# Attention steps with the transposes of a pair's probabilities ahead of the next pair's scores

## The reference

```python
q = (x @ wq).reshape(b, n, H, DH).transpose(0, 2, 1, 3)      # H = 16 heads of DH = 64
sim = jnp.einsum('bhid,bhjd->bhij', q, k) * SCALE
sim = jnp.where(mask[:, None, None, :], neg, sim)
attn = jax.nn.softmax(sim, axis=-1)
out = jnp.einsum('bhij,bhjd->bhid', attn, v)
return out.transpose(0, 2, 1, 3).reshape(b, n, INNER) @ wo + bo
```

## Time and profile before

| what | value |
|---|---|
| time, median of 3 runs | 1245.56 us (1244.93 to 1246.37) |
| the profiled execution's own time | 1244.36 us |
| its span, first to last instruction | 1242.6 us |
| TensorE busy | 1218.9 us (98%) |
| VectorE busy | 995.5 us (80%) |
| ScalarE busy | 875.4 us (70%) |
| GpSimd busy | 705.0 us (57%) |
| chain that ended last | TensorE 78%, VectorE 7%, ScalarE 5%, GpSimd 4% |

### The profile page before, as it was taken

The page is one execution under the profiler, slowest core; times in us unless marked ns, Lnnn a source line. Parts: engine busy times, 40 slices in busy tenths (PEclk is TensorE's granted clock), DMA queues, the critical chain, the costliest instruction groups (busy, mean ns, idle before and its releaser), DMA issues.

```text
span 1242.6 us, 31390 instructions
## 1 busy us (share of the span) xinstructions
PE 1218.9 (98%) x10415; PEld 1165.9 (94%) x10415; DVE 995.5 (80%) x2685; ACT 875.4 (70%) x2261; POOL 705.0 (57%) x1100
## 2 busy tenths in 40 slices
PE   8899999999999999999999999899999999999998
PEld 6899999999999999999999999899999999999898
DVE  6898988988989988888888888754454888888964
ACT  5788887888888888878878877544333776777642
POOL 4676656656678856555555578876515222334451
PEclk9999999999999999999999999999999999999999
DMA  6060000000000003200000010010004677877722
GB/s 195 2 244 22 2 18 19 2 18 19 2 27 27 2 27 121 77 27 27 2 27 27 2 36 27 27 49 30 1 20 152 224 267 270 267 247 249 264 82 92
DMA packets 74383, 100.60 MB, mean 81 GB/s; under 512 B 5616, under 2 KB 53616, under 8 KB 74224
## 3 DMA queue, kind: packets, MB, share of 16 engines
q1 hardware_dynamic: 72688, 94.40, 23.1%
q0 software_dynamic: 1536, 4.20, 1.1%
HBM read 84.16 MB, written 14.42 MB: 79 GB/s over the span
## 4 chain that ended last, share of the span: by engine, by line
PE 78%; DVE 7%; ACT 5%; issue 4%; POOL 4%; DMA 1%; POOLq 0%; DVEq 0%; ACTq 0%
PE ps_pj L52 9%; PE ps_pj L54 9%; PE ps_pj L53 9%; PE ps_t L949 8%; PE ps_s L939 8%; PE ps_pv L962 8%; PE ps_aux L52 3%; PE ps_aux L54 3%; PE ps_aux L53 3%; ACT probs L1268 3%; PE ps_s L52 3%; PE ps_s L54 3%; PE ps_s L53 3%; PE ps_pv L54 2%; PE ps_pv L53 2%
## 5 line engine op out<-in xcount | busy, mean ns | idle before, releaser
L666 POOL TENSOR_SCALAR probs<-probs,inv 128x256 f32<-128x256 f32 x512 | 237.2, 483 | 224.1 <-DVE inv L1512 223.4
L1268 ACT ACTIVATE probs<-scores,nb 128x256 f32<-128x256 f32 x512 | 253.6, 497 | 18.4 <-DVE nb L1502 17.9
L1502 DVE CUSTOM_DVE_ANT_0 scores<-ps_s,maskf 128x256 f32<-128x256 f32 x512 | 186.8, 421 | 51.3 <-PE ps_s L939 49.2
L1275 ACT ACTIVATE probs_t_hi<-ps_t 128x512 fp32r<-128x512 f32 x256 | 150.8, 590 | 103.4 <-PE ps_t L949 103.4
L1516 DVE TENSOR_TENSOR probs_t_lo<-ps_t,probs_t_hi 128x512 fp32r<-128x512 f32 x256 | 173.1, 676 | 0.2
L949 PE MATMUL ps_t<-ident,probs 128*128 128x128 f32 x1024 | 139.9, 279 | 0.6 <-POOL probs L666 0.6
L962 PE MATMUL ps_pv<-probs_t_lo,v_stack 128*128 128x256 f32 x512 | 130.6, 287 | 0.8 <-issue 0.7
L962 PE MATMUL ps_pv<-probs_t_hi,v_stack 128*128 128x256 f32 x512 | 127.8, 282 | 0.0
L949 PEld LDWEIGHTS ps_t<-ident,probs 128*128 128x128 f32 x1024 | 109.7, 141 | 17.8 <-POOL probs L666 0.9
L52 PE MATMUL ps_pj<-xq_hi,wq_lo 128*128 128x256 f32 x368 | 115.3, 313 | 3.3 <-POOL wk_lo L713 3.2
L685 POOL TENSOR_TENSOR heads_t_lo<-joined,heads_t_hi 128x256 fp32r<-128x256 f32 x128 | 95.1, 743 | 33.4 <-ACT heads_t_hi L1284 33.0
(11 more groups left out here) (285 smaller groups left out, 4480.6 us busy)
## 6 DMA issues: line engine op xcount, KB each, us to landing
raw<-in_L_ffn_W SPq DMA_DIRECT2D x96, 512.0 KB, 4.7
slot_rows<-hin SPq DMA_DIRECT2D x3, 768.0 KB, 5.9
rows<-in_x SPq DMA_DIRECT2D x8, 256.0 KB, 2.7
after_self<-rows SPq DMA_DIRECT2D x8, 256.0 KB, 2.1
rows<-after_self SPq DMA_DIRECT2D x8, 256.0 KB, 2.8
cin<-in_ctx SPq DMA_DIRECT2D x8, 256.0 KB, 3.0
after_cross<-rows SPq DMA_DIRECT2D x8, 256.0 KB, 2.2
stage<-in_L_xattn_fc_w SPq DMA_DIRECT2D x2, 1024.0 KB, 9.3
```

The source lines that it names most:

```text
L666: last = pool.tensor_scalar(PR[:, h, t, :], PR[:, h, t, :], inv[:, h, t:t + 1], 1.0, ALU.mult, ALU.mult)
L1268: last = act.activation(PR[:, h, t, :], SM[:, h, t, :], ACT.Exp, bias=nb[:, h, t:t + 1], scale=-1.0, accum_out=sums[:, h, t:t + 1])
L1275: act.activation(flat(PT[0][:, i % 2, h, :, :]), ps_t[h][:, :], ACT.Copy).then_inc(t_hi, 1)
L1502: last = dve.tensor_tensor_reduce(SM[:, h, t, :], ps_s[h][:, t * S:(t + 1) * S], maskf[:, i // PAIRS % 2, :], -SCALE, -LOWEST, ALU.add, AL ...
```

## The change

In steps 2 to 126 of TensorE's loop, the scores of the next pair are issued behind the two transposes of this pair's probabilities, not ahead of them. Steps 0, 1 and 127 keep the order. The other engines' queues are the same.

```diff
@@ -1165,7 +1165,8 @@
             for i in range(NPAIR + 3):
                 if i == 1:
                     project_qk(i + 2)
-                if i + 1 < NPAIR:
+                turned_first = 2 <= i < NPAIR - 1
+                if i + 1 < NPAIR and not turned_first:
                     scores(i + 1)
                 if i == 0:
                     project_qk(i + 2)
@@ -1177,6 +1178,8 @@
                 if i < NPAIR:
                     transpose_probs(i, 0)
                     transpose_probs(i, 1)
+                if turned_first:
+                    scores(i + 1)
                 if i >= 2 and i + 2 < NPAIR:
                     project_qk(i + 2)
                 if i >= 4 and i % 2 == 0:
```

## The result

The changed kernel takes 1345.88 us (median of 4 runs, 1344.22 to 1346.06) against 1245.82: a ratio of 1.080, 95% interval 1.078 to 1.082. Slower by 100 us, where 82 were forecast. The profiled execution took 1345.81 us, with a span of 1344.1.

The account below looks back on a forecast made before the run. TensorE's order bounds the kernel; after the change, a loop of 1.28+0.81+3.87+0.06+0.50, taken as 6.51 us, does. 119 steps plus 5 us late steps give 80.9 more, the start 1: 82 more, median 1327 us, range 1298 to 1350.

Parts of the forecast that it names:

- The loop: From one start of scores on TensorE to the next, through lo_of_probs(i,1) and the second head's transposes: 6.51 us a step.
- S to M: From the start of scores(i+1) on TensorE to the start of masked_max(i+1) on VectorE: 1.28 us.
- M to E: From the start of masked_max(i+1) on VectorE to the start of exps(i+1) on ScalarE: 0.81 us.
- E to the end of lo_of_probs: From the start of exps(i+1) on ScalarE to the end of lo_of_probs(i,1) on VectorE: 3.87 us.
- To TensorE: From the end of lo_of_probs(i,1) on VectorE to TensorE's waiting second-head transposes: 0.06 us.
- The transposes with the switch: On TensorE, the second head's four transposes and the switch to the scores: 0.50 us, ends 0.35 and 0.64.
- late steps on VectorE: Weight casts and row statistics ahead of masked_max make about ten steps 0.5 us late: 5 us, bounds 2 and 9.
- For the start: Six changed steps before scores(8), where TensorE waits for weights: 1 us more, bounds -3 and 4.
- The first: Rival: GpSimd's normalisations set the loop, 6.28 us a step, 1300 us; chance 0.06.
- The second: Rival: TensorE remains the bound, the loop taking under 5.76 us: 1241 to 1245 us; chance 0.05.
- The third, the clock: Rival: waits of 0.75 us a step lower TensorE's granted clock: 89 us more, 1416; chance 0.04.
- The fourth, late steps adding up: Rival: VectorE's and GpSimd's extra work delays more than ten steps: 1340 to 1360 us; chance 0.05.

Follow-up runs that it names:

- second experiment: Changed kernel with GpSimd normalising only the first column of each head's probabilities (outputs not those of the reference): 1345.6 us in one run.
- third experiments: Changed kernel with the second head's hi/lo_of_probs ahead of the qk parts on ScalarE and VectorE, and only the first column normalised: 1280.31 us in one run.
- the fourth: Changed kernel with scores(i+1) issued between the two heads' transposes, so behind the first head's only: 1246.6 us, ratio 1.000.
- the fifth: Changed kernel with the new order in even steps only, the old order in odd ones: 1273.2 us, ratio 1.0226.
- sixth experiment: Changed kernel with transpose_probs waiting first for lo_of_probs, then for the normalisation, instead of the other way round: 1338.25 us, ratio 1.0751.
- the first: Changed kernel with the second head's hi_of_probs and lo_of_probs ahead of the qk parts on ScalarE and VectorE: 1301.15 us, ratio 1.0436.

## Why the prediction was right, point by point

**The bound.** It was read rightly: TensorE's order set the pace, with 1.1 us of slack before the second head's transposes. The change used up that slack and 0.9 us beyond it (6.67 against 5.76).

**The loop.** S to M was taken as 1.28 and measured 1.27, M to E 0.81 and 0.81, E to the end of lo_of_probs 3.87 and 3.88. That it closes through lo_of_probs(i,1) is shown by the second and third experiments, that it needs the second head by the fourth, and that its full price falls only where changed steps follow each other by the fifth.

**What was mis-sized.** The two last terms. To TensorE: 0.06 taken, from the wait of the scores; 0.12 measured to the load. In the sixth experiment the order of the waits alone gave the 0.06 back. The transposes with the switch: 0.50 taken as the middle of 0.35 and 0.64; after the wait it is 0.59 from the load to S. Together 0.15 us, and 0.01 that was rounded off the sum of 6.52: 0.16 us in 119 steps are 19 us, and this is the gap between 1327 and 1345.88.

The switch itself was not the error. In the fourth experiment, where nothing waits, it is 0.53 us from the first transpose to the scores (562.66 to 563.19), close to the 0.52 that the prediction made from 0.43 and 0.09. The other 0.06 go with the wait. Where nothing waits, the load of the first transpose starts 0.10 us ahead of its matmul (562.56), while matmuls before it still run. After a wait TensorE has been idle, and from that load to S it was 0.59 us in the changed kernel as well as in the first and the sixth experiment (611.48 after 610.90 is 0.58 by the rounded starts). No row from before the change shows transposes behind a wait.

The Trainium skill, "TensorE: Matmul & The Clock Gate", section "Part 3: Packing small matmuls — row/col tiling", states that a load overlaps matmuls in flight only where row groups differ. The prediction made 0.64 us and 17 us more of it. The trace does not give the 0.64: transposes and switch took 0.53 us without a wait and 0.59 with one. Nor does it agree for full-width matmuls, whose row groups are the same: this load begins while the matmul before it still runs, by the profile's modelled end.

```profile
603.42 0.28 PE L54 MATMUL ps_pj<-xq_hi,wq_hi 128*128 128x256 f32 x1
```

```profile
603.54 0.19 PEld L53 LDWEIGHTS ps_pj<-xq_lo,wq_hi 128*128 128x128 f32 x1
```

**The range.** The step of 6.67 us lies outside the ends of the sum, 6.36 to 6.65, and outside the sign "6.4 to 6.65 us apart": the term of 0.06 was given no bounds. The time came to lie within 1298 to 1350, 4 us under the top, because the range also had room for 9 us of late steps, of which 1.7 came. That part is luck. Another sign came only by half: the wait before the transposes is put down to VectorE for the matmul, but to GpSimd for the load, and it took the second experiment to show that VectorE was meant.

**Smaller terms.** For late steps on VectorE 5 us were set down, and it was 1.7 (119 x 6.67 = 793.7 of 795.4). The row that the 5 us came from showed a lateness gathered over three steps: before, M was 1.52, 2.03 and then 2.56 us after S. With 0.9 us more in each step it no longer gathers, and M is late in 2 of the 119 steps, by 0.37 us. For the start 1 us was set down, and scores(8) came 4.1 us later. Of these, 0.4 lie ahead of scores(2), where the order is the old one (21.53 and 21.96), and 3.7 in the six changed steps, within the upper bound of 4: the step with the wait for wk_lo got only 0.6 us shorter (10.14 against 10.73 us), of 2.96 us of waiting, and the steps around it lost 0.7 to 0.9 each. These two errors nearly cancel.

**The rivals.** The first, that the normalisations set the loop at 6.28 us and 1300, did not hold for this change, but came true once lo_of_probs was moved away: 6.29 us and 1301. The second (TensorE stays the bound) is what the half exchange shows: 1246.6. The third, the clock: from 67.6 to 863 us it was 1.00, with TensorE waiting 0.7 us in every step:

```profile
67.60:863.00 795.40, 726.56 (x6281) 663.51 (x6280) 613.99 (x1991) 579.42 (x1631) 442.58 (x783) 1.00 0.09 30
```

The Trainium skill, "TensorE: Matmul & The Clock Gate", section "A second HAM failure mode: psum-queue depth-cycling", tells of a clock that swings in another kernel; with idle times of 0.7 us this trace shows no such swing. The fourth, late steps adding up, is refuted by the 1.7 us, although the time lies in its range of 1340 to 1360.

No version here is faster than the kernel before. The best of the new orders, one head only, ties with it, for both are bound by TensorE at 5.76 us a step.

## What to carry to other kernels

Before a producer's work is queued behind a consumer's on an in-order engine, write down the loop that this closes, from one start of the producer to the next, with every queue that it passes, and compare it with the busy time of a step: an engine that is 99% busy can still be made to wait by an order of its own. Look for the earliest point at which the exchange still leaves the loop short; here one of two heads was free and the second cost 100 us. And where a wait has two releasers, compare their ends with the start, since the waits view may name the one that had long been there.

## What the runs showed of the hardware that was not expected

Two waits ahead of one load on TensorE cost different times by their order. Where the semaphore that comes last was the wait written second, the load began 0.12 us after it (608.13 to 608.25); where it was written first and the other was already met, 0.06 us (610.84 to 610.90; 591.84 to 591.90 with the other releaser). In a loop that closed about 120 times this was worth 7 us: 100.1 us over the kernel before became 93.0.

The trace also shows where the two waits sit. The one written second is an instruction of its own in the queue of the loads, in the changed kernel that of `wait` (L418) for lo_of_probs, in the sixth experiment that for the normalisation (L946):

```profile
L418 PEldq EVENT_SEMAPHORE  x1: 51/51/51, 608.2 to 608.2; - x1
```

```profile
L946 PEldq EVENT_SEMAPHORE  x1: 51/51/51, 610.5 to 610.5; - x1
```

It takes 0.05 us (51 ns). In the changed kernel it lies between the end of lo_of_probs and the load, in the sixth experiment ahead of that end. That fits both the 0.06 us and the name in the view, which is that of the other wait, the one on the load; that it is the cause is not shown further.

Four transposes and the switch to matmuls of 64 rows took 0.53 us between matmul starts where nothing waited (562.66 to 563.19), and 0.59 us from the load where it had waited (608.25 to 608.84, 591.90 to 592.49); four transposes followed by full-width matmuls took 0.35 between starts.
